# ScalarE's copies behind a slot's activations, and the tail's first stack and block loads in another order

## The reference, cut to what matters

```
# block 0: x (16, 32, 28, 28), 192 hidden channels, ternary weights
x = relu6(bn(conv1x1(x, ternarize(w1)), g1, b1, m1, v1))     # 32 -> 192
x = relu6(bn(conv3x3(x, ternarize(w2)), g2, b2, m2, v2))     # 192 -> 192
x = x_in + bn(conv1x1(x, ternarize(w3)), g3, b3, m3, v3)     # 192 -> 32
# ternarize: delta = 0.7 * mean|w|, alpha = mean of |w| over the kept entries,
#            alpha * sign(w) where |w| > delta, else 0
# block 1: two 3x3 convolutions 32 -> 32, input and weights rounded to 8 bits by
#          the maximum of the whole tensor; batchnorm, relu; the second adds its input
# blocks 2 and 3: relu(bn(conv3x3(x) + conv_b)), 32 -> 32; a channel of an image
#          whose absolute maximum is under 1e-3 becomes 0
```

## Time and profile before

| what | value |
|---|---|
| median of three runs | 271.41 us |
| the profiled execution, its own time | 271.47 us |
| its span in the trace | 269.5 us |
| TensorE busy | 241.1 us, 89% |
| VectorE busy | 242.5 us, 90% |
| ScalarE busy | 195.2 us, 72% |
| GpSimd busy | 11.5 us, 4% |
| granted TensorE clock | full but for the last of 40 slices |

### The profile page before, as it was taken

How to read it: one execution, slowest core, us unless ns; L and a number is a source line. 1 busy time by engine, 2 the same in 40 slices (tenths; PEclk the granted TensorE clock), 3 DMA queues, 4 the chain that set the end, 5 groups by cost and what they waited for, 6 DMA issues and landing times.

```text
span 269.5 us, 5621 instructions
## 1 busy us (share of the span) xinstructions
PE 241.1 (89%) x2159; PEld 133.1 (49%) x2159; DVE 242.5 (90%) x473; ACT 195.2 (72%) x288; POOL 11.5 (4%) x30
## 2 busy tenths in 40 slices
PE   0649989998999989899999999999988999889992
PEld 0315554555554545455555555455534555445541
DVE  5799799999999999999999999899878858999894
ACT  5799876977756886777467868888433738998962
POOL 4800000000000000000000000000000000000003
PEclk9999999999999999999999999999999999999998
DMA  7528100200012000002100000000000000275306
GB/s 233 101 55 238 44 1 15 77 0 0 2 37 55 1 2 1 2 0 67 26 0 4 0 0 2 0 4 0 2 0 1 2 0 0 62 154 108 87 21 238
DMA packets 7098, 11.09 MB, mean 41 GB/s; under 512 B 2176, under 2 KB 5216, under 8 KB 7072
## 3 DMA queue, kind: packets, MB, share of 16 engines
q1 hardware_dynamic: 6880, 10.69, 14.9%
q10 hardware_dynamic: 192, 0.04, 0.1%
HBM read 4.04 MB, written 1.61 MB: 21 GB/s over the span
## 4 chain that ended last, share of the span: by engine, by line
DVE 44%; PE 23%; ACT 16%; issue 12%; DMA 2%; SPq 1%; DVEq 0%; ACTq 0%
PE ps L462 6%; ACT hs L783 5%; PE ps L639 5%; DVE hs L1149 4%; DVE ug L1142 4%; ACT ra L761 4%; PE ps L493 4%; PE ps L472 4%; DVE vv L1167 3%; DVE vv L1160 3%; PE ps L482 2%; DMA big<-w2b_in 2%; DVE ps L1188 2%; DVE vv L1166 2%; ACT big L968 2%
## 5 line engine op out<-in xcount | busy, mean ns | idle before, releaser
L761 ACT ACTIVATE ra<-ps,bn 128x392 f32<-128x392 f32 x64 | 42.6, 673 | 21.9 <-PE ps L440 20.9
L783 ACT ACTIVATE hs<-ug,magic 128x784 f16<-128x784 f16 x32 | 30.3, 952 | 17.7 <-DVE ug L1142 17.6
L472 PE MATMUL ps<-vv,w2at 128*128 128x392 f16 x192 | 37.9, 333 | 0.0
L462 PE MATMUL ps<-vv,wu 128*128 128x392 f16 x180 | 35.5, 332 | 0.0
L676 PE MATMUL ps<-big,wst 128*32 128x392 f16 (+2 forms) x576 | 25.6, 333 | 3.5 <-DVE big L1484 1.9
L440 PE MATMUL ps<-xk,w1t 96*128 96x392 bf16 x60 | 20.2, 348 | 9.0 <-ACT ra L761 5.4
L639 PE MATMUL ps<-qi,wqi 128*128 128x392 bf16 (+2 forms) x144 | 25.0, 333 | 0.7 <-ACT qi L936 0.7
L472 PEld LDWEIGHTS ps<-vv,w2at 128*128 128x128 f16 x192 | 18.4, 97 | 13.0 <-issue 1.0
L462 PEld LDWEIGHTS ps<-vv,wu 128*128 128x128 f16 x180 | 17.4, 97 | 11.0
L676 PEld LDWEIGHTS ps<-big,wst 128*32 128x32 f16 x576 | 14.8, 96 | 14.4 <-DMA big<-big 2.7
L472 PE MATMUL ps<-vv,w2bt 128*128 128x392 f16 x96 | 21.5, 333 | 0.0
(11 more groups left out here) (215 smaller groups left out, 428.3 us busy)
## 6 DMA issues: line engine op xcount, KB each, us to landing
xk<-xpart SPq DMA_DIRECT2D x45, 49.0 KB, 1.9
xin<-x_in SPq DMA_DIRECT2D x4, 392.0 KB, 3.8
big<-part SPq DMA_DIRECT2D x25, 56.2 KB, 2.0
big<-big SPq DMA_DIRECT2D x3, 450.0 KB, 3.9
y_out<-xin SPq DMA_DIRECT2D x3, 392.0 KB, 2.4
big<-w2a_in SPq DMA_DIRECT2D x3, 288.0 KB, 4.5
big<-w2b_in SPq DMA_DIRECT2D x6, 144.0 KB, 4.6
y_out<-xin SPq DMA_DIRECT2D x2, 196.0 KB, 2.3
```

The lines of the kernel that those rows point to most:

```text
L462: i = nc.tensor.matmul(ps[:, PBANK[k], :HALF], weights(s, k, dx, False), moving(s, k, dx, b), start=(s == 0 and dx == 0), stop=(s == 2 and ...
L472: i = nc.tensor.matmul(ps[:, PBANK[k], :HALF], weights(s, k, dx, False), moving(s, k, dx, b), start=False, stop=(s == 2 and dx == 2), skip ...
L761: nc.scalar.activation(dst[:, HALF * h:HALF * h + HALF], ps[:, bank, :HALF], ACT.Relu, bias=bn[:, BSH, at:at + 1], scale=bn[:, BSC, at:at ...
L783: nc.scalar.activation(inner(hs[:, 2 * two]), img(ug[:, two, :]), ACT.Identity, bias=magic[:, 2:3]).then_inc(hh_ready, 1)
```

## The change

1. **Loads.** SP waits until w2b's first half has landed, then issues the second half, then w3; before, it issued w3 and the second half without a wait.
2. **Front on ScalarE and TensorE.** The square of w2at goes ahead of the four `relu_exp(1, ...)`; the square of w2bt goes into slot 0; `x_high(1, 0)` goes behind slot 0. TensorE no longer runs eight warming matmuls ahead of the last six of the first `middle`; in slot 0 `total(4)` stands behind `middle(1)`, and the last `expand` behind `middle(2)`.
3. **Slots on ScalarE.** `x_high` and the first `integer_block` stand behind `relu_exp(j + 2, 1)` and `(j + 2, 2)` instead of ahead of them; the two copies of x for a chunk are spread over two slots.
4. **Tail.** ScalarE makes two blocks of stack (0,0) instead of three (VectorE makes one more) and does so ahead of `shifted(2)`; VectorE doubles that stack ahead of `q_lo(1)`. SP issues only the first two blocks of a stack; the others, nine in all, are issued by GpSimd, each with a semaphore of its own, and whoever waited for the blocks waits for these as well (`landed`).

```diff
-A_COUNT = ((3, 2, 3, 2), (3, 3, 2, 2))
+A_COUNT = ((2, 2, 3, 2), (3, 3, 2, 2))
+SP_COUNT = 2
...
+        def landed(eng, layer, c):
+            eng.wait_ge(s_hi[layer][c], 16 * min(SP_COUNT, len(D_BLOCKS[layer, c])))
+            for s in s_soft[layer][c]:
+                eng.wait_ge(s, 16)
...
                 sp.dma_start(w2br[0:HB, dy], w2b[:, dy]).then_inc(s_w2b, 16)
+            sp.wait_ge(s_w2b, 48)
+            for k in range(3):
+                dy = slice(3 * HID * k, 3 * HID * k + 3 * HID)
+                sp.dma_start(w2br[HB:P, dy], w2b[:, dy]).then_inc(s_w2c, 16)
             sp.dma_start(w3r[:, 0, :], w3[0:P]).then_inc(s_w3, 16)
...
-            for k in range(3):
-                dy = slice(3 * HID * k, 3 * HID * k + 3 * HID)
-                sp.dma_start(w2br[HB:P, dy], w2b[:, dy]).then_inc(s_w2c, 16)
...
-                for g, k in D_BLOCKS[layer, c]:
+                for g, k in D_BLOCKS[layer, c][:SP_COUNT]:
...
+            for layer, c in ((0, 0), (0, 1), (0, 2), (1, 0), (0, 3), (1, 1), (1, 2), (1, 3)):
+                if len(D_BLOCKS[layer, c]) > SP_COUNT:
+                    pool.wait_ge(part_ready[layer], 2 * c + 1)
+                    stack_free(pool, layer, c)
+                for n, (g, k) in enumerate(D_BLOCKS[layer, c][SP_COUNT:]):
+                    pool.dma_start(kst[C * k:C * k + C, KBUF[layer][c], g].rearrange("p h w -> p (h w)"),
+                                   part[C * g:C * g + C, layer, c % 2, k].rearrange("p h w -> p (h w)")).then_inc(s_soft[layer][c][n], 16)
...
                 if s == 2:
-                    warm(8)
                     pe.wait_ge(w2_ready, 3)
...
-                if split is not None:
-                    x_high(split, 1)
-                if after is not None:
-                    integer_block(after, 0)
                 if ahead:
                     relu_exp(j + 2, 1)
                     relu_exp(j + 2, 2)
+                if split is not None:
+                    x_high(*split)
+                if after is not None:
+                    integer_block(after, 0)
...
             slot(0, 0, first=True)
-            slot(0, 1, first=True, split=1)
-            x_high(2, 0)
-            slot(0, 2, first=True)
-            slot(0, 3, first=True, split=2)
+            x_high(1, 0)
+            slot(0, 1, first=True, split=(1, 1))
+            slot(0, 2, first=True, split=(2, 0))
+            slot(0, 3, first=True, split=(2, 1))
...
             shifted(1)
+            stack(0, 0)
             shifted(2)
-            stack(0, 0)
             stack(0, 1)
...
             q_hi(1)
+            dup(0, 0)
             q_lo(1)
-            dup(0, 0)
```

More of the change, by code:

```diff
@@ L192, in conv_seq @@
         s_hi = [[sem(f"s_hi{l}_{k}") for k in range(NCH)] for l in range(2)]
+        s_soft = [[[sem(f"s_soft{l}_{k}_{n}") for n in range(len(D_BLOCKS[l, k][SP_COUNT:]))] for k in range(NCH)]
+                  for l in range(2)]
         s_out = sem("s_out")
@@ L328, in dup @@
             def dup(layer, c):
-                sp.wait_ge(s_hi[layer][c], 16 * len(D_BLOCKS[layer, c]))
+                landed(sp, layer, c)
                 sp.wait_ge(stack_v[layer], c + 1)
@@ L524, in slot @@
                     outer(3, j, b)
-                    pe.wait_ge(a_sum, 4)
-                    total(4, 2, col[:, PART1 + 1:PART1 + 5:3], col[:, PART2 + 1:PART2 + 5:3])
                 if ahead:
@@ L534, in slot @@
                 if begin:
+                    pe.wait_ge(a_sum, 4)
+                    total(4, 2, col[:, PART1 + 1:PART1 + 5:3], col[:, PART2 + 1:PART2 + 5:3])
                     expand(j + 2, 2)
-                if ahead:
+                elif ahead:
                     expand(j + 2, 3)
                 middle(2, j + 1, b1)
+                if begin:
+                    expand(j + 2, 3)
                 if last and g == G - 2:
@@ L819, in slot @@
                     relu_exp(j + 2, 0)
+                    act.wait_ge(w2_ready, 3)
+                    act.wait_ge(a_sum, 3)
+                    nc.scalar.activation(wjunk[0:HB, :], w2bt[0:HB].rearrange("p t o -> p (t o)"), ACT.Square,
+                                         accum_out=col[0:HB, PART2 + 4:PART2 + 5]).then_inc(a_sum, 1)
                 else:
@@ L871, in _ @@
                                  accum_out=col[:, PART1 + 1:PART1 + 2]).then_inc(a_sum, 1)
+            act.wait_ge(a_sum, 1)
+            nc.scalar.activation(ajunk, w2at[:].rearrange("p t o -> p (t o)"), ACT.Square,
+                                 accum_out=col[:, PART1 + 4:PART1 + 5]).then_inc(a_sum, 1)
             for quarter in range(4):
@@ L876, in _ @@
                                  accum_out=col[0:HB, PART2 + 1:PART2 + 2]).then_inc(a_sum, 1)
-            x_high(1, 0)
-            act.wait_ge(w2_ready, 2)
-            act.wait_ge(a_sum, 1)
-            nc.scalar.activation(ajunk, w2at[:].rearrange("p t o -> p (t o)"), ACT.Square,
-                                 accum_out=col[:, PART1 + 4:PART1 + 5]).then_inc(a_sum, 1)
-            act.wait_ge(w2_ready, 3)
-            act.wait_ge(a_sum, 2)
-            nc.scalar.activation(wjunk[0:HB, :], w2bt[0:HB].rearrange("p t o -> p (t o)"), ACT.Square,
-                                 accum_out=col[0:HB, PART2 + 4:PART2 + 5]).then_inc(a_sum, 1)
             copy_m1(0)
@@ L911, in _ @@
             slot(1, 1)
-            x_high(3, 0)
-            slot(1, 2)
-            slot(1, 3, split=3)
+            slot(1, 2, split=(3, 0))
+            slot(1, 3, split=(3, 1))
             slot(2, 0)
@@ L1461, in halves_l @@
                     dve.wait_ge(stack_a[layer], c - 1)
-                    dve.wait_ge(s_hi[layer][c - 2], 16 * len(D_BLOCKS[layer, c - 2]))
+                    landed(dve, layer, c - 2)
                 return [inner(part[:, layer, c % 2, k]) for k in range(2)]
@@ L1478, in dup @@
                 dve.wait_ge(stack_a[layer], c + 1)
-                dve.wait_ge(s_hi[layer][c], 16 * len(D_BLOCKS[layer, c]))
+                landed(dve, layer, c)
                 first = LROWS[LAST][0] + 2 if (layer, c) == LAST else H + 2
```

## The result

The changed kernel takes **270.2 us** (median of 13 runs, 269.34 to 270.75) against 271.41 for the kernel before (13 runs beside them, 271.15 to 273.44). The ratio is 0.9943, with a 95% interval of 0.9925 to 0.996: faster by 1.2 us, where the forecast was 1.3 (270.1). The profiled execution took 269.87, with a span of 268.1 against 269.5. So of the trace 1.45 us has to be explained.

The account below looks back on a forecast made before the run. VectorE's unbroken run was taken as the bound to 171 us, then a tail woven of several engines. Gains 1.66 - 0.2 + 0.25 + 0.2 + 0.4 = 2.3, less tail 0.6 + 0.4 = 1.0: 1.3 faster, 270.1 us, range 268.9 to 271.6.

Parts of the forecast that it names:

- Front: Ahead of the first seeds: ScalarE's new order and eight fewer warming matmuls start VectorE's seeds 1.66 us sooner.
- Slot 0: VectorE's scales newly wait 0.2 us for TensorE's total, at full cost.
- Weight load: Third w2b load lands sooner without six loads issued behind it: 0.25 us gained, between bounds of nothing and 0.7.
- Middle: VectorE from 30 to 171 us: gains the 0.2 us for which it waited for TensorE.
- Slots 12 and 13: An integer block behind two ra removes TensorE's waits of 0.43 and 0.26; 0.4 us of 0.69 kept.
- the 1.19: VectorE's wait at 171.61 for ra, behind two other integer blocks; forecast to stay.
- Tail, 0.6: ScalarE's low copy of image 1 waits for q_lo(1), now behind the doubling; 0.6 us reaches the end.
- The wait of 0.41 ahead of the doubling of (1,1): VectorE's wait at 253.14 for SP's late blocks; forecast to fall away, so VectorE's added 0.40 doesn't reach the end.
- GpSimd's first blocks: Doubling of (0,0) waits for two GpSimd blocks: 0.4 us taken; lower end cost 0, upper 3.7.
- Rival 2: GpSimd's first blocks late, VectorE stands at the doubling; slower overall from a wait of 1.7 us; chance 0.15.
- Rival 1: Tail free: ScalarE swallows its 0.75, blocks land by 231.6, the 2.3 us stay, 269.1; chance 0.22.
- rival 3: Front: VectorE's earlier run meets late data, 1.0 of 2.3 us is left, the tail eats it, 271.4; chance 0.13.

Follow-up runs that it names:

- first two experiments: Kernel before without its eight warming matmuls: 271.26 us; changed kernel with these eight put back: 270.48 us.
- the run that brings it back: Changed kernel with the x copies and first integer block of a slot ahead of the two ra again: 270.62 us.
- the old tail: Changed kernel with the tail of the kernel before (three ScalarE blocks of the first stack, old order, SP issues every block): 269.19 us, ratio 0.9919.

## Why the prediction was right, point by point

The sum came out with some luck. The front and the body were forecast at 2.3 and gave 2.07, the tail was forecast to cost 1.0 and cost 0.62, so two terms that were too large stood against each other; and of the 2.07, 0.34 was a difference between two runs. The way of the front and of the slots was right, the way of the tail was not.

- **Front.** Right, and both parts were needed (first two experiments). The seeds stood at 27.27 where the sum gave 27.2. The step "late next is VectorE itself" holds only when TensorE's clock rises early. I took the 25.85 of one trace as fixed; it moves with the 18 matmuls ahead of it by over a us.
- **Slot 0.** The wait is the one forecast, its size was off for the same reason: 0.45 in the view and 0.55 of the lead, instead of 0.2. In the traces with an early rise or 12 matmuls 0.23 to 0.24 of the lead goes there, the 0.2 of the forecast, though no view prints a wait.
- **Weight load.** The landing came sooner by 0.56 (9.49, 8.93), but 0.25 was too much for what passes on: 0.04 at most. The term that failed is the cover. I looked at ScalarE's own work (until 8.75) and not at GpSimd's, which ends at about 11.8 to 12.1 and holds the scaling of bn. The second half of w2b had landed by 13.2, long before 16.39.
- **Middle.** Right: 0.2, shown by the run that brings it back.
- **Slots 12 and 13.** 0.4 forecast, 0.48 measured, all of it behind the last seeds by way of the wait for cy, and not where I put it. That the 1.19 stays, and what it waits for, was right.
- **Tail, 0.6.** The number was right and the step behind it wrong. ScalarE's copy is late as worked out (231.66 + 2.07 is 233.73, forecast 233.7), and it doesn't reach the end. What does is 0.37 of a hole in VectorE's queue, and 0.24 of ScalarE's order, VectorE's added block, which I had let fall away, and the added waits together.
- **The wait of 0.41 ahead of the doubling of (1,1)** did not fall away, it is 0.36. SP still issues two of the four blocks, right behind the 450 KB doubling of (0,3), and the second of them lands at 251.19, last of all. GpSimd's second block of this stack took 5.3 us and landed at 251.00, when VectorE's copies ended: "2 us and more to spare" did not hold for it.
- **GpSimd's first blocks.** 0.4 was too much, it is 0. They land 2.2 and 2.0 us after their issues at 226.29 and 227.07, ahead of 229.53; the lower end was right. Rival 2 is out.
- **Rival 1** (the tail is free) did not happen, though both its conditions did: ScalarE's late copy is swallowed and the blocks are there by 231.6. It would take the old tail (269.19); **rival 3** did happen in part: 0.55 of the front was given back in slot 0.
- **Range.** All 13 runs lie in 268.9 to 271.6.

## What to carry over

When a wait goes, ask what stands behind it not only in this trace but over several: TensorE was covered by some 0.7 us and has a spread of 1.5 of its own, which one trace can't show. Compare lengths between two fixed instructions rather than whole times, and test a term even where the sum comes out: here a right 0.6 had a wrong cause. And waits are instructions: adding some of them to a queue moves everything behind them, also to places where the engine stalls.

## What the runs showed of the hardware

- **TensorE's rise from 1.2 to 2.4 GHz** comes at a point that differs by some 2.9 us from run to run, with the same program up to there (18 matmuls in 4.10 to 5.57 us).
- **A delay of 0.4 us in VectorE's queue** at a fixed place of its stream, behind the 574th or 575th instruction in the record: one or two instructions less ahead of a place take it away from there, and in the traces with the old tail it lies under a long operation. The page of the profile has queues of their own for loads of instructions. One of them, q14, moves a packet of 8 KB 0.6 to 0.9 us behind the end of this delay in each of the 13 traces that show the delay: at 253.8 in the changed kernel (delay over at 253.10), at 257.2 in the kernel before (256.47). That fits a fetch of instructions; that the delay is one is argued, and no run tests it.
- **A small VectorE operation held by a GpSimd memset.** The scaling of bn (128x2) takes 0.22 us at the least and up to 0.93, and in all 14 traces it ends 0.22 to 0.26 behind the end of one memset. In the changed kernel, GpSimd's and VectorE's rows:

```profile
10.46 1.34 POOL L407 MEMSET part<- 128x448 f16 x1
11.24 0.79 DVE L1101 TENSOR_SCALAR bn<-bn,col 128x2 f32<-128x2 f32 x1
```

  The memset ends at 11.80, the scaling at 12.03. The Trainium skill's "SBUF — State Buffer", section "Who interferes with whom", has such a lock between the two, for whoever comes second; the trace agrees that VectorE can be the one that waits, even for 256 values.
- **DMAs issued by GpSimd** land about as fast as SP's beside them, also with VectorE's copies running: blocks of 56 KB from its queue and from SP's in the changed kernel (size, median us to landing).

```profile
big<-part SPq DMA_DIRECT2D x16, 56.2 KB, 2.3
big<-part POOLq DMA_DIRECT2D x9, 56.2 KB, 2.4
```

  The 0.8 that the prediction held against them, by the rule of the same section of the Trainium skill, did not show: the second block of (0,0) was issued at 227.07, over VectorE's two copies at 227.03, took 0.51 to issue and landed after 1.99. Behind the 450 KB doubling both issuers' blocks are slow: there the median is 4.4 for GpSimd's three and 3.6 for SP's four (244 to 254 us), and SP's blocks in the kernel before have 2.0 over all 25.
